# Queries and keys turned by the DMA engines' transpose instead of TensorE's, in a one-core transformer block

## The chip, the cores and the metric

The kernel runs on one core of a Trainium2 chip (trn2). The metric is the device time in microseconds of one execution. Before the change it was 766.03 us, the median of three runs (764.91 to 766.18). The core has five engines with instruction queues of their own: TensorE (PE, with its weight loads listed as PEld), VectorE (DVE), ScalarE (ACT), GpSimd (POOL) and SyncE (SP), which here only issues DMAs.

## The reference, cut to what matters

```python
x = x + 0.5 * ffn(layernorm(x))          # x: 8 x 512 x 128
x = x + attn(layernorm(x))
x = x + 0.5 * ffn(layernorm(x))
# attn: 16 heads of 64
q = rmsnorm(x @ Wq, q_rms_w);  k = rmsnorm(x @ Wk, k_rms_w);  v = x @ Wv
gate   = softplus(einsum('bthd,hd->bht', k, u / |u|) / sqrt(64))
bias   = -dist * softplus(omega) * slopes * gate         # causal
scores = q @ k.T / sqrt(64) + bias
y      = softmax(scores) @ v @ Wproj
```

`rmsnorm` divides each head's 64 numbers by their root mean square and multiplies them by a weight of 64 numbers.

## The kernel before, in words

The eight batches are worked off one after the other, each software-pipelined into the next. The order of the work on every engine is written out by hand in `ORDER` (line 27): one list per engine for the lead-in, the first batch, the six middle batches ("body", b = 1 to 6), and the last one. Each entry is a stage with its numbers and THIS, NEXT or LAST for the batch that it belongs to, so one body period works on three batches. An engine takes its own list strictly in order, and a wait at its head holds up all behind it. The stages of attention are grouped in four quarters (`qd`, four heads each) and four token blocks (`t`, 128 tokens).

To keep nearly full precision with 16-bit products, an operand is split into an upper part (rounded to 16 bits) and a lower part (what is left). `product` (lines 1087 to 1089) makes three matmuls of such pairs. PE's results of most stages go through a ring of four PSUM banks (`RING`); `taken_by` gives a bank back.

The way of queries and keys before:

- `qk`: PE projects one token block of a quarter, 512 columns. ACT squares it (L975) and copies it in 32 bits to `qkn` (L976), which gives the bank back; DVE sums the squares per head (L1551). `qkn` holds two quarters, eight blocks.
- `qkn`: ACT takes logarithm and exponential to get one over the root (L984, L987); POOL multiplies (L869).
- `t`: PE transposes with the 32-bit identity (`turn_heads`, L1200), 16 transposes of 128x128 for two banks of queries and two of keys per quarter. ACT writes the upper parts times the RMS weights into `qk2` (`hi_parts`, L1023), DVE subtracts for the lower parts (`lo_parts`, L1576), both reading PSUM. There are eight `t` stages per batch, eight transposes each.
- SP then copies by DMA: `rows` puts the upper parts into `qk1` (`place_upper`, L652, two of 256 KB a quarter), `swap` and `back` (L750, L751, L755, L756, four of 128 KB a quarter) arrange both halves of `qk2`.
- `gr`/`gd`/`nm` bring the gate rows and the negated row maxima into `qk1`. `a` (L1218, DVE L1586) finds row maxima, `s` (L1244 to L1246, ACT L1048) makes scores and exponentials.
- `pl`: POOL makes the lower part of the exponentials (L843); in the last batch DVE makes one of three (L1500). `pv` is the product with the values, DVE divides by the sums (L1601), ACT and POOL split it (`yt`, L1063, L847), and SP turns it by a DMA transpose (L766, 256 KB each, one per pair of heads).

Elsewhere DVE subtracts with both inputs in SBUF at a few places: L1434 (32 rows of the normed input), L1490 (hidden layer in the first and last feed-forward) and L1500. Its other large operations, L1576 and L1608 among them, read one input from PSUM. In the lead-in POOL makes the bias rows (`b2`, L892 to L897) and the diagonal of `u` (`ud`, L830).

```python
def place_upper(eng, qd, n):
    eng.dma_start(qk1[0:D, qd, n, :, :, :], qk2[n * D:(n + 1) * D, qd, K1:Q0 + 1, :, :])
# lo_parts, DVE, for each of queries and keys, 128 x 512, bank in PSUM
scalar_tensor_tensor(qk2[..LOWER..], bank, w, qk2[..UPPER..], ALU.mult, ALU.subtract)
# exponentials_lo, for comparison: both inputs in SBUF
tensor_tensor(pt_l[..], pt[..], pt_h[..], ALU.subtract)
```

Of the kernel before, what the change touches and what calls it, by code (L numbers as in the profile page):

```python
# [6 lines left out]
ALU = mybir.AluOpType  # L7
# [27 lines left out]
            ("t", 3, NEXT), ("qk", 2, 1, NEXT), ("qk", 2, 2, NEXT), ("a", 0, NEXT), ("qk", 2, 3, NEXT),
            ("a", 1, NEXT), ("qk", 3, 0, NEXT), ("a", 2, NEXT), ("a", 3, NEXT), ("v", 0, 2, NEXT), ("qk", 3, 1, NEXT),
            ("nm", 0, NEXT), ("qk", 3, 2, NEXT), ("a", 4, NEXT), ("v", 0, 3, NEXT), ("qk", 3, 3, NEXT),
            ("a", 5, NEXT), ("s", 0, NEXT), ("a", 6, NEXT), ("s", 1, NEXT), ("gl", 1, NEXT), ("a", 7, NEXT),
            ("t", 4, NEXT), ("v", 1, 0, NEXT), ("nm", 1, NEXT), ("pv", 0, NEXT), ("t", 5, NEXT), ("t", 6, NEXT),
        ],  # L40
        "first": [
            ("s", 2, THIS), ("t", 7, THIS), ("gr", 1, THIS), ("pv", 1, THIS), ("v", 1, 1, THIS), ("s", 3, THIS),
            ("pv", 2, THIS), ("a", 8, THIS), ("s", 4, THIS), ("a", 9, THIS), ("pv", 3, THIS), ("zt", "a", NEXT),
            ("s", 5, THIS), ("m", "a", NEXT), ("pv", 4, THIS), ("a", 10, THIS), ("s", 6, THIS), ("a", 11, THIS),
            ("h", "a", NEXT), ("nm", 2, THIS), ("wp", 0, THIS), ("pv", 5, THIS), ("out", "a", NEXT),
            ("v", 1, 2, THIS), ("s", 7, THIS), ("v", 1, 3, THIS), ("s", 8, THIS), ("a", 12, THIS),
            ("zt", "att", NEXT), ("pv", 6, THIS), ("a", 13, THIS), ("qk", 0, 0, NEXT), ("qk", 0, 1, NEXT),
            ("qk", 0, 2, NEXT), ("qk", 0, 3, NEXT), ("pv", 7, THIS), ("s", 9, THIS), ("a", 14, THIS),
            ("qk", 1, 0, NEXT), ("pv", 8, THIS), ("a", 15, THIS), ("qk", 1, 1, NEXT), ("v", 0, 0, NEXT),
            ("v", 0, 1, NEXT), ("qk", 1, 2, NEXT), ("qk", 1, 3, NEXT), ("pv", 9, THIS), ("gl", 0, NEXT),  # L50
            ("nm", 3, THIS), ("v", 0, 2, NEXT), ("wp", 1, THIS), ("t", 0, NEXT), ("t", 1, NEXT), ("s", 10, THIS),
            ("v", 0, 3, NEXT), ("gr", 0, NEXT), ("s", 11, THIS), ("t", 2, NEXT), ("t", 3, NEXT), ("s", 12, THIS),
            ("pv", 10, THIS), ("a", 0, NEXT), ("qk", 2, 0, NEXT), ("pv", 11, THIS), ("a", 1, NEXT), ("s", 13, THIS),
            ("a", 2, NEXT), ("qk", 2, 1, NEXT), ("qk", 2, 2, NEXT), ("pv", 12, THIS), ("a", 3, NEXT),
            ("qk", 2, 3, NEXT), ("qk", 3, 0, NEXT), ("s", 14, THIS), ("a", 4, NEXT), ("qk", 3, 1, NEXT),
            ("pv", 13, THIS), ("nm", 0, NEXT), ("qk", 3, 2, NEXT), ("a", 5, NEXT), ("s", 15, THIS),
            ("qk", 3, 3, NEXT), ("wp", 2, THIS), ("a", 6, NEXT), ("gl", 1, NEXT), ("pv", 14, THIS), ("a", 7, NEXT),
            ("t", 4, NEXT), ("nm", 1, NEXT), ("t", 5, NEXT), ("t", 6, NEXT),
        ],
        "body": [  # L60
            ("pv", 15, LAST), ("t", 7, THIS), ("s", 0, THIS), ("v", 1, 0, THIS), ("v", 1, 1, THIS), ("gr", 1, THIS),
            ("s", 1, THIS), ("v", 1, 2, THIS), ("s", 2, THIS), ("pv", 0, THIS), ("wp", 3, LAST), ("zt", "a", NEXT),
            ("pv", 1, THIS), ("s", 3, THIS), ("m", "a", NEXT), ("pv", 2, THIS), ("a", 8, THIS), ("s", 4, THIS),
            ("pv", 3, THIS), ("v", 1, 3, THIS), ("s", 5, THIS), ("a", 9, THIS), ("h", "a", NEXT), ("s", 6, THIS),
            ("a", 10, THIS), ("wp", 0, THIS), ("pv", 4, THIS), ("a", 11, THIS), ("out", "a", NEXT), ("nm", 2, THIS),
            ("zt", "c", LAST), ("pv", 5, THIS), ("s", 7, THIS), ("a", 12, THIS), ("pv", 6, THIS), ("s", 8, THIS),
            ("zt", "att", NEXT), ("pv", 7, THIS), ("a", 13, THIS), ("qk", 0, 0, NEXT), ("s", 9, THIS),
# [230 lines left out]
def macaron(nc: bass.Bass, x, Wq, Wk, Wv, Wproj, q_rms_w, k_rms_w, omega, u, W1, b1, W2, b2, scale, out):  # L298
# [23 lines left out]
    with ExitStack() as ctx:  # L322
# [147 lines left out]
        def q2(h):  # L470
            return qk2[:, h // QH, Q2[h % 2], h % QH // 2, :]
# [1172 lines left out]
```

## Time and profile before

| | |
|---|---|
| three runs | 764.91, 766.03, 766.18 us |
| the profiled execution | 766.36 us, of which the span from first to last instruction is 764.6 us |
| granted TensorE clock over the span | 0.991 of full |
| body | six periods of about 88.9 us |
| before the body | 75 us lead-in, then the first batch |

The profile gives for each engine the time in which an instruction of it ran (busy), for groups of equal instructions their number, mean duration and the idle time ahead of them, and for stretches of the span the same sums. Engines pipeline: an instruction's duration can overlap the next one's, so start-to-start distances in the timeline are what an instruction costs its engine when it is followed at once.

### The profile page before, as it was taken

The page shows a single profiled execution, that of the slowest core. Times are in us where ns is not written, and L with a number is a line of the kernel's source. Part 1 is how long each engine was busy: PE and PEld are TensorE (multiplying, and loading weights), DVE is VectorE, ACT ScalarE, POOL GpSimd, SP SyncE. Part 2 cuts the span into 40 slices and gives each one's busy share as a digit, 9 for nine tenths or more (in the row PEclk, how much of TensorE's full clock was granted, in tenths as well). Part 3 has the DMA queues.
Part 4 walks back from the last instruction along what each step waited for, and adds up shares of the span by engine and source line. Part 5 has one row for each costly group of instructions (what it writes and reads, how often), then busy time and mean ns, then how long its engine had stood idle before and what let it go on. Part 6 is the DMA issues. An engine that isn't in the chain of part 4 may idle for free.

```text
span 764.6 us, 25092 instructions
## 1 busy us (share of the span) xinstructions
PE 734.0 (96%) x9298; PEld 528.4 (69%) x9298; DVE 660.0 (86%) x2105; ACT 640.4 (84%) x1420; POOL 645.3 (84%) x753
## 2 busy tenths in 40 slices
PE   4889999999999999999999999999999999999987
PEld 2455777677667777587667776577776876777765
DVE  8799878987989788887989879898898879899976
ACT  5687889888998889987998889988898889986673
POOL 6356879989998989989999899989899899997791
PEclk9799999999999999999999999999999999999999
DMA  7022513343243423454053432535134440534431
GB/s 200 13 67 48 126 31 87 84 86 86 44 112 72 85 60 71 91 108 100 3 126 72 86 86 44 113 72 107 38 76 95 99 99 16 113 72 101 98 44 30
DMA packets 99618, 60.33 MB, mean 79 GB/s; under 512 B 74622, under 2 KB 86400, under 8 KB 99496
## 3 DMA queue, kind: packets, MB, share of 16 engines
q1 hardware_dynamic: 99336, 58.19, 35.8%
q8 instruction: 75, 1.23, 0.7%
q10 hardware_dynamic: 160, 0.52, 0.2%
q14 instruction: 47, 0.39, 0.2%
HBM read 4.74 MB, written 2.10 MB: 9 GB/s over the span
## 4 chain that ended last, share of the span: by engine, by line
PE 73%; ACT 11%; DVE 9%; issue 3%; POOL 2%; DMA 1%; SPq 0%; DVEq 0%; ACTq 0%; POOLq 0%
PE ps L1087 13%; PE ps L1088 13%; PE ps L1089 13%; PE ps L1218 8%; PE ps L1244 7%; PE ps L1245 7%; PE ps L1200 5%; ACT qk L1023 3%; PE ps L1246 3%; ACT pt L1048 2%; DVE masked L1586 2%; PE ps L1104 1%; ACT hid L965 1%; POOL pt_l L843 1%; PE ps L1114 1%
## 5 line engine op out<-in xcount | busy, mean ns | idle before, releaser
L843 POOL TENSOR_TENSOR pt_l<-pt 128x512 f16<-128x512 f32 x366 | 321.5, 907 | 35.1 <-ACT pt L1048 33.4
L1586 DVE CUSTOM_DVE_ANT_0 masked<-ps,causal_row 128x512 f16<-128x512 f32 x448 | 192.1, 486 | 26.2 <-PE ps L1218 25.3
L1048 ACT ACTIVATE pt<-ps 128x512 f32<-128x512 f32 (+1 forms) x384 | 174.7, 535 | 17.5 <-PE ps L1246 14.5
L869 POOL TENSOR_TENSOR qkn<-qkn,rs 128x512 f32<-128x512 f32 x128 | 129.9, 1043 | 29.3 <-ACT rs L987 28.6
L1244 PE MATMUL ps<-qk 128*128 128x512 f16 (+3 forms) x512 | 146.7, 300 | 0.0
L1245 PE MATMUL ps<-qk 128*128 128x512 f16 (+3 forms) x512 | 146.6, 299 | 0.0
L1087 PE MATMUL ps<-v_buf,pt 128*128 128x65 f16 x1280 | 129.8, 194 | 2.6 <-POOL pt_l L843 1.2
L1088 PE MATMUL ps<-v_buf,pt 128*128 128x65 f16 x1280 | 129.8, 194 | 0.0
L1089 PE MATMUL ps<-v_buf,pt_l 128*128 128x65 f16 x1280 | 129.6, 194 | 0.0
L1087 PEld LDWEIGHTS ps<-v_buf,pt 128*128 128x128 bf16 x1280 | 118.0, 98 | 8.4 <-issue 4.9
L1088 PEld LDWEIGHTS ps<-v_buf,pt 128*128 128x128 bf16 x1280 | 117.5, 98 | 1.8
L1089 PEld LDWEIGHTS ps<-v_buf,pt_l 128*128 128x128 f16 x1280 | 117.5, 97 | 0.0
L1246 PE MATMUL ps<-causal_t,ident 128*128 128x128 f16 x512 | 105.7, 219 | 0.0
L1218 PE MATMUL ps<-qk 96*128 96x512 f16 (+3 forms) x512 | 97.0, 300 | 1.8 <-ACT qkn L976 0.5
L847 POOL TENSOR_TENSOR ytt<-ytok,ytt 128x512 f16<-128x512 f32 x63 | 74.1, 1177 | 19.9 <-ACT ytt L1063 18.4
L975 ACT ACTIVATE sq<-ps 128x512 f32<-128x512 f32 x128 | 77.6, 606 | 13.7 <-PE ps L1089 13.1
L1551 DVE TENSOR_REDUCE ss<-sq 128x8 f32<-128x512 f32 x128 | 82.8, 679 | 5.4 <-ACT sq L975 5.2
L976 ACT ACTIVATE qkn<-ps 128x512 f32<-128x512 f32 x128 | 78.2, 611 | 0.0
L1087 PE MATMUL ps<-wqkv_h,zt_h_att 128*128 128x512 f16 x192 | 74.1, 386 | 4.0 <-DVE qk L1576 1.9
L1088 PE MATMUL ps<-wqkv_l,zt_h_att 128*128 128x512 f16 x192 | 73.8, 384 | 0.0
L1089 PE MATMUL ps<-wqkv_h,zt_l_att 128*128 128x512 f16 x192 | 73.6, 384 | 0.0
L1218 PEld LDWEIGHTS ps<-qk 96*128 96x128 f16 x512 | 44.1, 97 | 40.0 <-issue 4.4
(212 smaller groups left out, 1968.8 us busy)
## 6 DMA issues: line engine op xcount, KB each, us to landing
qk<-qk SPq DMA_DIRECT2D x128, 128.0 KB, 2.4
qk<-qk SPq DMA_DIRECT2D x62, 256.0 KB, 3.7
x_in<-in_L_attn_x SPq DMA_DIRECT2D x8, 256.0 KB, 3.0
out<-x_out SPq DMA_DIRECT2D x7, 256.0 KB, 2.4
qk<-qk SPq DMA_DIRECT2D x1, 1024.0 KB, 8.1
qk<-gtt SPq DMA_DIRECT2D x64, 8.0 KB
qk<-nmt SPq DMA_DIRECT2D x64, 2.0 KB
y_hl<-ytt SPq DMA_TRANSPOSE x62, 3.2
```

The lines of the kernel that those rows point to most:

```text
L843: g.tensor_tensor(pt_l[:, h % 2, c], pt[:, h % 2, c], pt_h[:, h % 2, c], ALU.subtract).then_inc(s_pt_l, 1)
L869: g.tensor_tensor(qk, qk, r.unsqueeze(4).broadcast_to([P, 2, 2, 2, D]), ALU.mult).then_inc(s_qkn, 1)
L1048: a.activation(pt[:, h % 2, c], ps[:, j, 0:width], ACT.Exp).then_inc(s_exp, 1)
L1087: pe.matmul(dst, ah, bh, start=first, stop=False)
L1088: pe.matmul(dst, ah, bl, start=False, stop=False)
L1089: return pe.matmul(dst, al, bh, start=False, stop=last)
L1218: mm = pe.matmul(dst, q1(h)[0:MROW, ib * P:keys], k1(h)[0:MROW, 0:keys], start=True, stop=by_dve)
L1244: pe.matmul(dst, k1(h)[:, keys], q1(h)[:, kb * P:T], start=True, stop=False)
L1245: pe.matmul(dst, k2(h)[:, keys], q2(h)[:, kb * P:T], start=False, stop=False)
L1246: mm = pe.matmul(dst[:, 0:P], ident16[:, :], causal_t16[:, :], start=False, stop=True)
L1551: d.tensor_reduce(ss[:, :, qd % 2, t, :], sq[:, blk % 4, :].rearrange("p (j m d) -> p j m d", j=2, d=D), AX.X, ALU.add).then_inc(s_sqsum, 1)
L1586: ins = d.tensor_tensor_reduce(masked[:, part.unit(s, i)[0], col:col + (ib + 1) * P], part.bank(s, i)[:, col:col + (ib + 1) * P], causal_r ...
```

## The change

Queries and keys are split while they still lie by token, and DMA transposes bring them into the layout by head.

- ACT still squares the whole bank; it then copies the queries' half only (256 columns, scaled by 1/16). DVE multiplies the keys' half by the product of both RMS weights (they only meet in the dot product) into the same tile and gives the bank back.
- `qkn` holds 5 token blocks instead of 8; ACT's copy waits for the lower part of the block five before.
- POOL multiplies as before. ACT then copies `qkn` to 16 bits (upper), DVE subtracts from `qkn` for the lower part: four of each per quarter, as before, now with all inputs in SBUF. They go to `qk_hl`, 128 x 1024 per block in the order lower query, upper query, upper key, lower key.
- SP turns each block with one DMA transpose of 256 KB into `qk2`, which thereby has both arrangements; `swap` and `back` are gone. `rows` is four DMAs of 128 KB a quarter.
- PE's `t` stages (512 transposes) are gone, with their 128 uses of ring banks.
- All five orders are new. In the lead-in the 512-column matmuls that only keep PE busy are 10, 3 and 6 instead of 8 and 10 (6 more stay), POOL makes `b2` ahead of `m`, and `ud` waits for DVE's L1490.

The diff, cut to its core:

```diff
@@ vector order, body, second half @@
-            ("v", 0, 1, NEXT), ("gl", 0, NEXT), ("v", 0, 2, NEXT), ("pv", 9, THIS), ("t", 0, NEXT), ("t", 1, NEXT),
-            ("pv", 10, THIS), ("wp", 1, THIS), ("t", 2, NEXT), ("gr", 0, NEXT), ("v", 0, 3, NEXT), ("pv", 11, THIS),
+            ("qk", 0, 2, NEXT), ("qk", 0, 3, NEXT), ("pv", 8, THIS), ("a", 15, THIS), ("t", 0, NEXT),
+            ("qk", 1, 0, NEXT), ("qk", 1, 1, NEXT), ("m", "c", LAST), ("t", 1, NEXT), ("qk", 1, 2, NEXT),
...
@@ gpsimd order, lead @@
-            ("ul", NEXT), ("clear", NEXT), ("m", "a", NEXT), ("b2", NEXT), ("ud", NEXT), ("wvl", NEXT), ("wol", NEXT),
+            ("ul", NEXT), ("b2", NEXT), ("m", "a", NEXT), ("clear", NEXT), ("ud", NEXT), ("wvl", NEXT),
...
@@ sync order, body @@
+            ("ln1", "a", NEXT), ("gd", 2, THIS), ("rows", 2, THIS), ("yt", 7, LAST), ("tq", 6, THIS), ("tq", 7, THIS),
+            ("gd", 3, THIS), ("yt", 0, THIS), ("yt", 1, THIS), ("rows", 3, THIS), ("nm", 2, THIS), ("yt", 2, THIS),
+            ("yt", 3, THIS), ("nm", 3, THIS), ("tq", 0, NEXT), ("tq", 1, NEXT), ("rows", 0, NEXT), ("gd", 0, NEXT),
+            ("tq", 2, NEXT), ("tq", 3, NEXT), ("gd", 1, NEXT), ("yt", 4, THIS), ("rows", 1, NEXT), ("yt", 5, THIS),
+            ("tq", 4, NEXT), ("add", "c", LAST), ("nm", 0, NEXT), ("tq", 5, NEXT), ("yt", 6, THIS), ("nm", 1, NEXT),
...
-        qkn = sb("qkn", [P, 2, 4, 2, T // 2])
+        TOKENS = 5
+        qkn = sb("qkn", [P, TOKENS, 512])
+        qk_hl = sb("qk_hl", [P, TB, 2 * 512], F16)
...
-        def place_upper(eng, qd, n):
-            eng.dma_start(qk1[0:D, qd, n, :, :, :], qk2[n * D:(n + 1) * D, qd, K1:Q0 + 1, :, :]).then_inc(s_upper[qd % 2], 16)
+        def place_upper(eng, b, qd, j):
+            for t in range(TB):
+                eng.wait_ge(s_qk_turned[t], (b * 4 + qd + 1) * 16)
+            side, rows = ((HI_LO, slice(0, D)), (LO_HI, slice(D, P)))[j]
+            for n in range(2):
+                eng.dma_start(qk1[0:D, qd, n, j, :, :], qk2[rows, qd, n::2, side, :]).then_inc(s_upper[qd % 2], 16)
...
+            def turn_qk(part, s, b, p):
...
+                if b > 0:
+                    sp.wait_ge(s_s_ps, ((b - 1) * H + (qd + 1) * QH) * 3)
+                for t in (2 * th, 2 * th + 1):
+                    sp.wait_ge(s_lo, block_of(b, qd, t) + 1)
+                    sp.dma_start_transpose(qk2[:, qd, :, :, t * P:(t + 1) * P].rearrange("p m j c -> p (m j) c"),
+                                           qk_hl[:, t, :]).then_inc(s_qk_turned[t], 16)
...
             def diagonal_u(part, s, b):
                 pool.wait_ge(s_u_unit, 1)
+                pool.wait_ge(s_hid_l_dve, FB)
...
             def take_qk(part, s, b, qd, t):
...
-                part.taken_by(a.activation(tokens(qd, t), part.bank(s).rearrange("p (j i n) -> p j i n", j=2, i=2), ACT.Copy), s)
+                if blk >= TOKENS:
+                    act.wait_ge(s_lo, blk - TOKENS + 1)
+                a.activation(of_q_and_k(tokens(blk), 0), part.bank(s)[:, 0:256].rearrange("p (m d) -> p m d", d=D),
+                             ACT.Copy, scale=1.0 / QKV_UP).then_inc(s_q_out, 1)
...
             def hi_parts(part, s, b, p):
...
+                    a.activation(upper(t), tokens(blk).rearrange("p (m f) -> p m f", m=QH), ACT.Copy).then_inc(s_hi, 1)
...
             def square_sums(part, s, b, qd, t):
...
+                dve.wait_ge(s_q_out, blk + 1)
+                part.taken_by(d.tensor_tensor(of_q_and_k(tokens(blk), 1), part.bank(s)[:, 256:512].rearrange("p (m d) -> p m d", d=D),
+                                              kw[:, :].unsqueeze(1).broadcast_to([P, QH, D]), ALU.mult), s)
...
             def lo_parts(part, s, b, p):
...
+                    dve.wait_ge(s_hi, blk + 1)
+                    d.tensor_tensor(lower(t), tokens(blk).rearrange("p (m j d) -> p m j d", m=QH, j=2),
+                                    upper(t).rearrange("p m (j d) -> p m j d", j=2), ALU.subtract).then_inc(s_lo, 1)
```

## Rows read from the trace of the kernel before

**Rows 1.** The page's busy shares of the whole span.

```profile
PE 734.0 (96%) x9298; PEld 528.4 (69%) x9298; DVE 660.0 (86%) x2105; ACT 640.4 (84%) x1420; POOL 645.3 (84%) x753
```

**Rows 2.** Busy time by stretch, five body periods; then the sum over them.

```profile
core 0: us, PE busy (x) PEld busy (x) DVE busy (x) ACT busy (x) POOL busy (x), PEclk, DMA share, GB/s
254.75:344.07 89.32, 88.42 (x1154) 64.05 (x1151) 77.15 (x261) 79.22 (x180) 81.13 (x93) 1.00 0.41 79
...
sum 444.29, PE 441.94 PEld 320.26 DVE 385.88 ACT 395.94 POOL 404.74; mean PE 88.39 PEld 64.05 DVE 77.18 ACT 79.19 POOL 80.95
```

**Rows 3.** Who waited for whom in those five periods: PE, DVE and POOL.

```profile
PE ps L1087 <- DMA y_hl<-ytt: 0.6, 1, 0.6
...
DVE masked L1586 <- PE ps L1218: 21.0, 35, 1.6
...
POOL pt_l L843 <- ACT pt L1048: 17.8, 25, 1.3
```

**Rows 4.** Busy time of line L1200 alone (PE's transposes) in the same five periods.

```profile
166.06:610.35 444.29, 41.66 (x320) 34.31 (x320) 1.00 0.38 80
```

**Rows 5.** Groups of ACT instructions by line: busy, mean ns.

```profile
L976 ACT ACTIVATE qkn<-ps 128x512 f32<-128x512 f32 x128 | 78.2, 611 | 0.0
...
L1063 ACT ACTIVATE ytt<-ytok 128x512 f16<-128x512 f32 x63 | 39.7, 631 | 3.8 <-DVE ytok L1601 3.3
...
L1023 ACT ACTIVATE qk<-ps,qws 128x512 f16<-128x512 f32 x64 | 45.0, 704 | 6.0 <-PE ps L1200 5.6
...
L952 ACT ACTIVATE zt_h_att<-ps 128x256 f16<-128x256 f32 x16 | 5.2, 376 | 0.0
```

**Rows 6.** DVE's timeline: start us, us; the distances of starts are what counts.

```profile
421.24 0.42 DVE L1601 TENSOR_TENSOR ytok<-ps,rden 128x256 f32<-128x256 f32 x1
421.58 0.74 DVE L1576 SCALAR_TENSOR_TENSOR qk<-ps,qws,qk 128x512 f16<-128x512 f32 x1
422.24 0.74 DVE L1576 SCALAR_TENSOR_TENSOR qk<-ps,kws,qk 128x512 f16<-128x512 f32 x1
```

**Rows 7.** DVE subtractions by line: ns min/median/max; L1500 and L1434 read SBUF twice.

```profile
L1500 DVE TENSOR_TENSOR pt_l<-pt x18: 681/967/1523, 690.3 to 740.5; 128x512 f16<-128x512 f32 x17, 128x256 f16<-128x256 f32 x1
...
L1434 DVE TENSOR_TENSOR z_hl<-z_a,z_hl x16: 281/282/697, 8.1 to 752.3; 32x128 f16<-32x128 f32 x16
...
L1608 DVE TENSOR_TENSOR v_buf<-ps,v_buf x64: 656/684/695, 42.1 to 710.3; 128x512 f16<-128x512 f32 x64
```

**Rows 8.** Timeline of POOL, then DVE, in the last batch: an overlap, and one without.

```profile
730.53 2.06 POOL L843 TENSOR_TENSOR pt_l<-pt 128x512 f16<-128x512 f32 x2 [0.39 <-ACT pt L1048]
...
702.72 1.61 POOL L843 TENSOR_TENSOR pt_l<-pt 128x512 f16<-128x512 f32 x2 [0.69 <-ACT pt L1048]
...
731.02 1.10 DVE L1500 TENSOR_TENSOR pt_l<-pt 128x512 f16<-128x512 f32 x1 [0.27 <-ACT pt L1048]
...
738.18 3.13 DVE L1500 TENSOR_TENSOR pt_l<-pt 128x512 f16<-128x512 f32 x3
```

**Rows 9.** Busy time by stretch, the part of the last batch with L1500.

```profile
690.00:742.00 52.00, 50.07 (x802) 38.54 (x800) 47.83 (x143) 35.65 (x77) 41.65 (x40) 1.00 0.41 82
```

**Rows 10.** The group of L1500 over the span: busy, mean ns.

```profile
L1500 DVE TENSOR_TENSOR pt_l<-pt 128x512 f16<-128x512 f32 (+1 forms) x18 | 16.9, 949 | 1.1 <-ACT pt L1048 1.1
```

**Rows 11.** SP's timeline: what issuing a transpose, and two copies, takes.

```profile
426.77 1.24 SPq L766 DMA_TRANSPOSE y_hl<-ytt  x1
428.06 1.23 SPq L652 DMA_DIRECT2D qk<-qk  x2
```

**Rows 12.** The page's DMA issues: count, KB each, median us from issue to landing.

```profile
qk<-qk SPq DMA_DIRECT2D x128, 128.0 KB, 2.4
qk<-qk SPq DMA_DIRECT2D x62, 256.0 KB, 3.7
...
y_hl<-ytt SPq DMA_TRANSPOSE x62, 3.2
```

**Rows 13.** DVE's and POOL's timeline in the lead-in.

```profile
17.34 5.12 DVE L1490 TENSOR_TENSOR hid_l<-hid 128x512 f16<-128x512 f32 x4 [1.16 <-ACT hid L965]
...
18.48 2.23 POOL L830 TENSOR_TENSOR pt<-usq,ident 16x1024 f32<-16x1024 f32 x1
```

More of the change, by code:

```diff
@@ L35 @@
[L35 to L39, printed above, removed]
+            ("out", "a", NEXT), ("warm", 1, 10, NEXT), ("zt", "att", NEXT), ("warm", 1, 3, NEXT), ("qk", 0, 0, NEXT),
@@ L783, in store @@
                         sp.dma_start(rows[:, TB // 2:TB, :], x_out[:, TB // 2:TB, :]).then_inc(s_out, 16)
[L785 removed]
+            run(ORDER["sync"], {"weights": load_weights, "clear": constant_rows, "ln1": load_x, "rows": place_operands, "gd": place_gates, "tq": turn_qk, "yt": turn_y, "nm": max_rows, "add": store})
             sp.wait_ge(s_out, 16 * (B + 1))
@@ L1016, in hi_parts, with place_queries @@
             def hi_parts(part, s, b, p):
-                if b == 0 and p == 0:
-                    act.wait_ge(s_prepared, 1)
-                    act.wait_ge(s_wv_lo, 1)
-                    act.wait_ge(s_wp_lo, 1)
-                for j, w in enumerate((qws, kws)):
-                    part.full(act, s, j)
-                    a.activation(qk2[:, p // 2, UPPER[j], p % 2, :], part.bank(s, j), ACT.Identity, scale=w[:, :]).then_inc(s_hi, 1)
-            def place_odd_heads(part, s, b, qd):
+                qd, th = p // 2, p % 2
+                for t in (2 * th, 2 * th + 1):
+                    blk = block_of(b, qd, t)
+                    act.wait_ge(s_qkn, blk + 1)
+                    if blk >= TB:
+                        act.wait_ge(s_qk_turned[t], (b * 4 + qd) * 16)
+                    a.activation(upper(t), tokens(blk).rearrange("p (m f) -> p m f", m=QH), ACT.Copy).then_inc(s_hi, 1)
+            def place_queries(part, s, b, qd):
                 if b == 0 and qd < 2:
@@ L1192, in gate_rows @@
                                             gt[:, :, :, :, :].rearrange("p s r i t -> p (s r i t)"), ident16[:, :]), s)
-            def turn_heads(part, s, b, p):
-                pe.wait_ge(s_qkn, (b * 4 + p // 2 + 1) * TB)
-                for j in range(2):
-                    part.room(pe, s, j)
-                    for t in range(TB):
-                        mm = pe.transpose(part.bank(s, j)[:, t * P:(t + 1) * P],
-                                          tokens(p // 2, t)[:, j, p % 2, :], ident[:, :])
-                    part.filled_by(mm, s, j)
             def max_scores(part, s, b, h):
```

474 lines of the change are left out of this document (235 added, 239 removed).

## The prediction

> **What bounds the kernel now.** I read the busy shares first: PE works 96% of the span, the other three 84 to 86% [rows 1]. The share is a mean over stages, so I cut the body into its periods. One lasts 88.86 us (444.29 over five), and in it PE is busy 88.39 us, POOL 80.95, ACT 79.19, DVE 77.18 [rows 2]. PE idles half a microsecond per period. The waits agree: in five periods one wait of PE itself counts, 0.6 us, while DVE waits 21 us for PE's maxima and POOL 17.8 us for exponentials that in turn wait for PE [rows 3]. So PE sets the pace, and whatever leaves PE is worth its time until the next engine is full. The reader should see how near that is: POOL has 7.9 us of room in a period, DVE 11.7.
>
> **What leaves PE.** The transposes keep it busy 41.66 us in five periods, 8.33 each (64 of 0.13 us) [rows 4]. PE's load falls to 80.1 us. The ring of banks has 16 uses fewer per batch; the bank of a `qk` stage is held about as long as before (square, a shorter copy, then DVE's 0.34 us), so I cost the ring at nothing.
>
> **ACT.** Per block it loses a copy of 0.611 us and an upper part of 0.704 us from PSUM, and gets a copy of 256 columns, like the 0.376 us one, and a cast from SBUF, like the 0.631 us one [rows 5]. That is 0.31 us less for each of 16 blocks, 4.9 us; ACT falls to 74.3. It now also waits at a copy for the lower part of five blocks before, with exponentials queued behind it. DVE's lists put the lower parts within five blocks of their own, so I add nothing, and keep it for the upper end.
>
> **DVE.** By distances of starts, the old lower part costs 0.66 us and a product of 256 columns 0.34 us [rows 6]. Out go 16 x 0.66 = 10.6 us; in come 16 x 0.34 = 5.4 us for the keys and 16 x 0.60 = 9.6 us for the new lower part (0.68 us alone, less the same 0.08 us of overlap as in those rows). Undisturbed, DVE rises from 77.2 to 81.7 us. That would leave the change a large gain.
>
> **The term that decides.** The new lower part reads SBUF twice, the old one read PSUM once. Compare DVE's subtractions of equal size: with one input in PSUM (L1608) 64 of them lie between 0.656 and 0.695 us, with POOL busy all the while. With both in SBUF (L1500) they lie between 0.681 and 1.523, median 0.967, and the small L1434 goes from 0.281 to 0.697 [rows 7]. The timeline shows against what: where POOL works, DVE's instruction takes 1.10 us, and POOL's pair of instructions, 1.61 us when undisturbed, takes 2.06; three such DVE instructions in a row take 3.13 us [rows 8]. So DVE waits until POOL's instruction is through, then POOL's next is held for 0.45 us; a second DVE instruction right behind finds POOL's next already in and waits again.
> The Trainium skill (SBUF — State Buffer, "Who interferes with whom") states this as a rule against this change: a DVE instruction with two SBUF inputs contends with a GpSimd one that reads SBUF, and the second to come is blocked until the first is finished. The rows agree on DVE's side; of the 0.68 us they show POOL losing 0.45. By the full 0.68 POOL would need 80.95 + 16 x 0.68 = 91.8 us.
>
> Price for DVE, per lower part: the low end is the mean of all 18, 0.949 - 0.681 = 0.27 us [rows 7, 10], measured where POOL was busy 80% (41.65 of 52.00) [rows 9] against 91% in the body. The high end is the longest, 1.523 - 0.681 = 0.84 us [rows 7]. The lower parts come in pairs, the second ready behind the first: I take 0.33 us for the first (0.27 scaled by POOL's higher share) and 0.67 for the second (near the high end, less where ACT has not yet made its upper part), mean 0.50. DVE: 81.7 + 16 x 0.50 = 89.7 us. POOL: 80.95 + 16 x 0.45 = 88.2 us. Both stand about where the period is today, 88.86 us, so PE's 8.3 us are bought with two engines that are full. The engine that bounds will not be without idle time: PE had 0.5 us, but its suppliers had 8 to 12 us of room. DVE's would have 1.5 (POOL), so I give it 1 us. Period 90.7 us, 1.8 more. Seven such periods (six of the body and the first batch, whose load is alike) make +13 us.
>
> **SP and the DMA queues.** Issuing a transpose takes 1.24 us, two copies 1.23 [rows 11]. A period has 16 transposes more (20 us), 8 copies more for `rows` (5) and 16 fewer of `swap` and `back` (10): SP issues some 15 us more, to about 50 of 88.9 us, by my count of its list. In the engines 16 transposes, 256 KB and 3.2 us each to landing, replace 16 copies of 128 KB at 2.4 us [rows 12]. Even if each kept all 16 engines for its whole landing time, 51 us of a period, with a DMA share of 0.38 to 0.41 now [rows 2], the sum would stay under full. On the path of a quarter stand 3.2 + 1.24 us of transposes and two more issues, some 5.7 us. PE's list has ten stages and more between the last projection of a quarter and its first maxima, and these cover it; the wait on the last batch's scores comes long after those. In a middle case this costs nothing; without cover it is 5.7 us a quarter.
>
> **Lead-in and end.** In the lead-in DVE's four hidden lower parts take 5.12 us while POOL makes the diagonal [rows 13]; undisturbed 4 x 0.60 + 0.08 = 2.5. The new wait puts that away, 2.6 us off a chain on which little else happens. Against it the first maxima wait for 4 to 6 us of transposes, in place of PE's transposes and, before the scores, of `swap` and `back`. I take -2.6, between -6 and +5. The end has none of the changed stages but `t` 7: nothing.
>
> **Sum.** 764.6 + 12.6 - 2.6 = 774.6 us of span. The profiled execution took 766.36 us, 1.8 around its span and 0.3 above the median of the runs. That makes 776.4, and against the median 776.
>
> **Rivals.** (1) *POOL's port has just room enough, and it is faster.* If lower parts mostly fall where POOL or DVE would have idled anyway, DVE is no bound and the floor is POOL's 88.2 us. It decides from 81.7 + 16w + 1 < 88.86, a mean wait w under 0.39 us, well inside my 0.27 to 0.84. Then -0.7 x 7 = -5, lead-in -3: 758, down to 755 with the lead-in at its best. For it: ACT and PE get room, so POOL's waits for exponentials shrink. Against it: POOL would have to be 99% busy, every period. Chance 0.27, 0.02 of it within 0.2% of today. (2) *The new instructions don't collide*, whatever L1500 did: DVE at 81.7 + 1 = 82.7 us, -6.2 x 7 - 3 = 720. Nothing in the rows speaks for it; 0.04. (3) *Each of a pair waits for a whole POOL instruction*: DVE 81.7 + 16 x 0.84 = 95.1 us at most; halfway from 90.7, a period of 92.8, +3.9 x 7 - 2.6 = 791. That is also about where the skill's full block of POOL, 91.8 and 1 idle, leads. Chance 0.12. (4) *Late quarters*: one of four uncovered in each period, 5.7 x 7 = +40, 804. SP takes its list in order, so a late lower part also holds y's transposes and the maxima behind it; 0.05. The forecast itself, 765 to 785, has 0.52, of which 0.05 within 0.2%.
>
> **The numbers.** A measurement of this kernel can tell 0.2%, 1.5 us, from no change. Faster: 0.25 + 0.04 = 0.29. The same: 0.07. Slower: 0.47 + 0.12 + 0.05 = 0.64. The range reaches from rival 1's low end to within rival 3: 753 to 796. It leaves out rivals 2 and 4, some of 3 and a little of 1, under 0.2 in all. Most of the slower cases alone lie between 768 and 794.
>
> **What would show each step.** PE busy near 80 us in a period, its idle time now several us, ended by DVE or POOL. The new lower part on DVE with a minimum of 0.68 and a mean near 1.18 us, the product of keys at 0.42 without spread. Some 16 POOL instructions a period 0.45 us longer than their like, as the pair of 2.06 against 1.61 us [rows 8]. DVE busy 98% of the body, POOL 96%. ACT near 74 us. L1490's four in 2.5 us. I am wrong if the lower parts stay at 0.68 us (rival 2), if DVE is under 95% busy while PE waits for a landing (rival 4), or if POOL's collisions are far fewer than 16 a period (rival 1).

## The result, and the profile after

The changed kernel takes 837.71 us (median of four runs, 835.62 to 841.32) against 765.47 for the kernel before in the same comparison: a ratio of 1.0948, 95% interval 1.0908 to 1.0988. It is 72 us slower, where 10 had been forecast and 796 was the upper end of the range. The profiled execution took 841.32 us with a span of 839.5 at a granted clock of 0.957 of the full 2.4 GHz.

The busy shares and the chain of waits, from the page of the changed kernel:

```profile
PE 720.5 (86%) x8787; PEld 486.9 (58%) x8787; DVE 749.3 (89%) x2232; ACT 621.3 (74%) x1421; POOL 692.5 (82%) x753
...
DVE 48%; PE 34%; issue 6%; ACT 4%; POOL 3%; DMA 3%; SPq 1%; DVEq 0%; ACTq 0%; POOLq 0%
```

Five body periods, each cut at the moment at which SP issues the load of the next input, from the busy time by stretch (PE, PEld, DVE, ACT, POOL, then granted clock, DMA share, GB/s):

```profile
269.72:366.03 96.31, 86.05 (x1086) 58.58 (x1084) 88.49 (x278) 76.78 (x178) 87.51 (x93) 0.98 0.50 95
...
464.07:562.40 98.33, 88.38 (x1086) 60.76 (x1084) 88.48 (x278) 76.96 (x179) 87.84 (x93) 0.95 0.53 94
...
sum 486.12, PE 432.70 PEld 295.02 DVE 442.05 ACT 384.77 POOL 437.39; mean PE 86.54 PEld 59.00 DVE 88.41 ACT 76.95 POOL 87.48
```

Cut in the same way, the kernel before has periods of 88.9 us, with PE 88.3, DVE 77.0, ACT 79.2 and POOL 81.1 (its [rows 2] were cut some 10 us later in the period and differ by 0.2 at most). In the changed kernel DVE is busy 88.4 us a period (forecast 89.7), POOL 87.5 (88.2), ACT 77.0 (74.3). Yet the period is 97.2 us (486.12 over five), not 90.7. No engine is full: DVE idles 8.8 us, POOL 9.7, PE 10.7. The reader should stop here: the two loads that were forecast came out within 1.3 us, and the period is 6.5 us longer than the sum made of them.

By line, DVE's new lower part, its product of the keys, and POOL's multiplication (ns, minimum, median and maximum); then a collision in the timeline (start us, us):

```profile
L1592 DVE TENSOR_TENSOR qk_hl<-qkn,qk_hl x128: 675/1098/1610, 37.7 to 763.3; 128x512 f16<-128x512 f32 x128
L1565 DVE TENSOR_TENSOR qkn<-ps,kw x128: 405/411/426, 29.3 to 748.3; 128x256 f32<-128x256 f32 x128
L889 POOL TENSOR_TENSOR qkn<-qkn,rs x128: 1047/1058/1522, 33.6 to 753.1; 128x512 f32<-128x512 f32 x128
```

```profile
314.69 3.00 DVE L1592 TENSOR_TENSOR qk_hl<-qkn,qk_hl 128x512 f16<-128x512 f32 x2
...
313.38 1.17 POOL L866 TENSOR_TENSOR ytt<-ytok,ytt 128x512 f16<-128x512 f32 x1
314.61 2.52 POOL L889 TENSOR_TENSOR qkn<-qkn,rs 128x512 f32<-128x512 f32 x2
```

The lower part has its minimum at 0.675 us and reaches 1.61; two of them take 3.00 us where POOL's pair takes 2.52 instead of the 2.08 that two lone multiplications take elsewhere. The product of the keys (L1565) has no spread at 0.41 us. The idle time, in the same five periods (us, times, longest):

```profile
ACT nmt L1078 <- PE ps L1238: 21.7, 10, 4.8
ACT qkn L998 <- DVE qk_hl L1592: 14.6, 20, 1.0
...
DVE rden L1613 <- PE ps L1111: 13.3, 10, 2.0
DVE x L1544 <- PE ps L1111: 9.5, 5, 1.9
...
PE ps L1136 <- DVE qkn L1565: 9.3, 5, 1.9
PE ps L1109 <- DVE qkn L1565: 8.0, 10, 1.4
PE ps L1230 <- DVE qkn L1565: 8.0, 15, 0.7
```

PE now waits 25.3 us for banks that DVE gives back after the keys' product (L1565), and ACT waits 14.6 us at the copy into the five-block buffer for a lower part. Before, PE's waits came to 0.6 us [rows 3]. DVE's waits for PE are no longer than they were: 22.8 us in the two groups shown and some 11 more in smaller ones, against 21.0 at the maxima [rows 3] and some 18 more in smaller groups before. What is new beside the banks is ACT's wait of 21.7 us for the turned row maxima (L1078), which was 2.2 us. It is still 16.6 us in a_free below, whose periods are as short as before, so by itself it need not lengthen a period.

Where the 74.9 us of span are, by the moment at which SP issues the load of each next input: lead-in 80.3 against 75.2 us (+5.1), the first batch 92.9 against 81.0 (+11.9), the five periods 486.1 against 444.6 (+41.6), everything after 180.2 against 163.8 (+16.4). The last figure holds the sixth body period too. If that one grew like the others, by 8 to 10 us, the last batch is left with 6 to 8; this split is an estimate from the other periods. So every stage with the changed work in it is longer, and the lead-in too, though its collision did go: L1490's four (now L1502) take 2.50 us for 5.12 [rows 13], and the first sums of squares start 2.8 us earlier (29.7 against 32.5), but the first exponentials 5.0 us later (72.2 against 67.2). Between these two points PE stands 4.7 us once at the first maxima for a copy of gate rows, and ACT 7.8 us for transposes that free `qk_hl`. One trace of each is not exact to the microsecond here: in kernels below whose lead-in is that of before, the first exponentials start between 64.7 (b_less_pool) and 67.3 us (b_half_v_turns).

### The profile page after: what moved, and what is told of

The parts are those of the page before. It is cut to its first block, busy times and chain, and to the rows that moved or that the text cites. A ratio compares the mean times of both kernels' runs of the same rounds, so it can differ in the third digit from the quotient of the medians.

```text
span 839.5 us, 24423 instructions
## 1 busy us (share of the span) xinstructions
PE 720.5 (86%) x8787; PEld 486.9 (58%) x8787; DVE 749.3 (89%) x2232; ACT 621.3 (74%) x1421; POOL 692.5 (82%) x753
## 3 DMA queue, kind: packets, MB, share of 16 engines
q8 instruction: 70, 1.15, 0.6%
## 4 chain that ended last, share of the span: by engine, by line
DVE 48%; PE 34%; issue 6%; ACT 4%; POOL 3%; DMA 3%; SPq 1%; DVEq 0%; ACTq 0%; POOLq 0%
DVE qk_hl L1592 12%; DVE masked L1602 10%; DVE ss L1568 8%; PE ps L1109 7%; PE ps L1111 6%; PE ps L1110 6%; DVE qkn L1565 4%; PE ps L1230 4%; PE ps L1255 3%; PE ps L1256 3%; DVE ytok L1617 3%; POOL pt_l L862 2%; DMA qk<-qk_hl 1%; PE ps L1126 1%; PE ps L1257 1%
## 5 line engine op out<-in xcount | busy, mean ns | idle before, releaser
L862 POOL TENSOR_TENSOR pt_l<-pt 128x512 f16<-128x512 f32 x366 | 344.0, 967 | 45.9 <-ACT pt L1070 45.7
L889 POOL TENSOR_TENSOR qkn<-qkn,rs 128x512 f32<-128x512 f32 x128 | 143.8, 1144 | 45.6 <-ACT rs L1010 44.6
L1109 PE MATMUL ps<-v_buf,pt 128*128 128x65 f16 x1280 | 135.0, 196 | 16.5 <-DVE ytok L1617 12.3
L1592 DVE TENSOR_TENSOR qk_hl<-qkn,qk_hl 128x512 f16<-128x512 f32 x128 | 142.1, 1148 | 2.7 <-ACT qk_hl L1046 2.6
L1109 PEld LDWEIGHTS ps<-v_buf,pt 128*128 128x128 bf16 x1280 | 121.0, 100 | 30.0 <-issue 20.2
L1110 PE MATMUL ps<-v_buf,pt 128*128 128x65 f16 x1280 | 135.0, 196 | 0.0
L1111 PE MATMUL ps<-v_buf,pt_l 128*128 128x65 f16 x1280 | 134.9, 196 | 0.0
L1230 PE MATMUL ps<-qk 96*128 96x512 f16 (+3 forms) x512 | 106.3, 318 | 24.7 <-DVE qkn L1565 12.7
L1110 PEld LDWEIGHTS ps<-v_buf,pt 128*128 128x128 bf16 x1280 | 120.6, 100 | 2.2
L1111 PEld LDWEIGHTS ps<-v_buf,pt_l 128*128 128x128 f16 x1280 | 120.5, 99 | 0.0
L1568 DVE TENSOR_REDUCE ss<-sq 128x8 f32<-128x512 f32 x128 | 86.0, 672 | 0.0
L1046 ACT ACTIVATE qk_hl<-qkn 128x512 f16<-128x512 f32 x128 | 75.6, 632 | 14.1 <-DMA qk<-qk_hl 7.8
L1230 PEld LDWEIGHTS ps<-qk 96*128 96x128 f16 x512 | 45.1, 101 | 67.3 <-issue 22.4
```

The source lines that it names most:

```text
L862: g.tensor_tensor(pt_l[:, h % 2, c], pt[:, h % 2, c], pt_h[:, h % 2, c], ALU.subtract).then_inc(s_pt_l, 1)
L889: g.tensor_tensor(qk, qk, r.unsqueeze(3).broadcast_to([P, QH, 2, D]), ALU.mult).then_inc(s_qkn, 1)
L1109: pe.matmul(dst, ah, bh, start=first, stop=False)
L1110: pe.matmul(dst, ah, bl, start=False, stop=False)
L1111: return pe.matmul(dst, al, bh, start=False, stop=last)
L1230: mm = pe.matmul(dst, q1(h)[0:MROW, ib * P:keys], k1(h)[0:MROW, 0:keys], start=True, stop=by_dve)
```

## The experiments

Theory A is the prediction's: DVE and POOL are full through collisions, and the period follows the fullest. Rivals: the bank that DVE gives back late; the DMA transposes' latency; the new orders; and later, that a period is no engine's load. Times are medians; each ratio is against the kernel before run beside it. The medians of that kernel lie between 763.5 and 765.7 us from one comparison to the next, so a difference of 2 us between two variants from different comparisons says nothing. Kernels made from the one before begin with b, from the changed one with a.

### Undoing parts of the change

```diff
# a_reduce_lo: DVE's lower part becomes a reduction of one input, no collision
-  d.tensor_tensor(lower(t), tokens(blk)..., upper(t)..., ALU.subtract)
+  d.tensor_reduce(<unused>, tokens(blk)..., AX.X, ALU.add)
# a_act_bank: ACT copies queries and keys and gives the bank back; DVE's product
# becomes a reduction of equal size that only POOL waits for
-  a.activation(of_q_and_k(tokens(blk), 0), part.bank(s)[:, 0:256]...)
+  part.taken_by(a.activation(tokens(blk)..., part.bank(s)...), s)
# a_both: both edits
# a_no_turn: no DMA transpose from the second batch on
+  if b == 0:
       sp.dma_start_transpose(qk2[...], qk_hl[:, t, :])
```

> The changed kernel with DVE's lower part (two inputs in SBUF) replaced by a sum over the same 512 numbers of the token block alone: one input in SBUF, 0.67 us like the other sums, same place, same waits. It leaves out the lower parts of queries and keys. If the collisions with POOL are the cause: DVE's load per body period falls from 88.4 to about 81.5 us, POOL's from 87.5 to 81, the period from 97.2 to 89 to 90, the time from 838 to 775 to 785. If the banks given back by DVE are: DVE and PE still wait for each other, the period stays above 93, the time at 810 to 825. If the DMA transposes come late: above 825.

> The changed kernel, but ACT copies all 512 columns of a qk bank and gives it back; DVE's instruction on 256 columns stays as a load of about the same length, but reads the keys' half of the token block in SBUF (a sum, one input), and POOL waits for it as before. It leaves out the RMS weights of the keys. The lower part still collides. If the collisions are the cause, the time stays within 825 to 840, since both engines keep their loads. If the banks given back by DVE are, PE's waits for that product (some 5 us a period) go and the time falls to 790 to 810.

> Both edits together (no lower parts, no weights of the keys). If the two causes explain the loss: DVE near 81.5 us per period, ACT near 79, and a period of 84 to 87, time 735 to 760. If the time stays above 800, the cause is neither: the transposes' path, the ring of five token blocks, or the orders themselves.

> The changed kernel without its DMA transposes from batch 1 on: SP waits as before for each lower part and for the scores, issues nothing, and what waited for a landing waits for the lower part instead. It leaves out the turning of queries and keys in batches 1 to 7, which then use those of batch 0. If the transposes' latency, their share of the DMA engines or SP's time are the cause, the time falls below 800. If the collisions or the banks are, it stays within 825 to 840.

What waited for a transpose that a_no_turn leaves out waits for the lower part instead. a_reduce_lo and a_both fill `qk_hl` with zeros once, on DVE in the lead-in.

Measured: a_reduce_lo 789.77 us, ratio 1.0314 (1.0264 to 1.0364); a_act_bank 845.74, 1.1068 (1.1034 to 1.1103); a_both 790.5, 1.0338 (1.0308 to 1.0367); a_no_turn 837.17, 1.0958 (1.0925 to 1.0991).

Taking the collisions away wins 48 us of the 72, though the 790 lies between what the two theories gave (775 to 785, and 810 to 825), and a_both, forecast at 735 to 760 or above 800, lies in neither. That DVE hands the bank back is not the main cause: with ACT doing it, PE's waits for L1565 are gone, but it now waits for other banks that come back late from DVE (14.0 us for L1623, 11.4 for the maxima L1601, in five periods), and the time is 8 us longer. The edit also puts 2.6 us a period more on ACT (79.6 for 77.0), so it does not show that the hand-back costs nothing. Transposes, with their issues on SP and their share of the queues, are worth nothing while the collisions are there. Without collisions, in a_reduce_lo:

```profile
sum 457.00, PE 420.15 PEld 287.69 DVE 403.01 ACT 380.27 POOL 407.42; mean PE 84.03 PEld 57.54 DVE 80.60 ACT 76.05 POOL 81.48
...
PE ps L1230 <- DMA qk<-qk: 10.4, 6, 2.9
```

Every engine is under 85 us and the period 91.4, still 2.5 longer than before. PE's maxima now wait for the copies of the upper parts, which come behind the transposes.

### Adding the suspected loads to the kernel before

```diff
# b_collide: the lower part reads its first input from SBUF (other values)
-  scalar_tensor_tensor(qk2[..LOWER..], part.bank(s, j), w[:, :], ...)
+  scalar_tensor_tensor(qk2[..LOWER..], w1s[:, :], w[:, :], ...)
# b_keys_op: 0.34 us of DVE work more per block, one input, its result unused
   dve.wait_ge(s_sq, blk + 1)
+  d.tensor_reduce(<unused>, w1s[:, 0:256]..., AX.X, ALU.add)
# b_loads: both
```

> The kernel before with only its lower part of queries and keys (L1576) reading a constant in SBUF instead of the PSUM bank, so both inputs in SBUF, same size, place and waits. It leaves out the true lower parts. PE keeps its transposes, and the order is that of before. If collisions cost DVE some 0.4 to 0.5 us and POOL 0.45 us each: DVE from 77.0 to about 83, POOL from 81.1 to about 88 us per period, the two still at or below the period of 88.9, and the coupled waits make it longer: 785 to 810. If collisions only hurt where the order has no room, this one has 8 to 12 us of it, and the time stays under 775.

> The kernel before with one more DVE instruction per token block of queries and keys, a sum of 256 numbers of a constant in SBUF, 0.34 us of DVE each, 5.4 us a period, one input, no collision, nobody waits for it. The output is whole. If DVE's load alone is the cause, the time rises by 15 us or more; if it is hidden in DVE's 11.9 us of idle time, by under 8 us.

> Both edits in the kernel before (it leaves out the true lower parts): DVE near 88 and POOL near 88 us per period, as in the changed kernel, but with PE's transposes, the old ring and the old order. If the loads and collisions make the changed kernel slow, this one is as slow or slower, 830 or more, for PE has 8 us more to do. If the new orders are at fault, it stays under 815.

Measured: b_collide 796.18, 1.0388 (1.0356 to 1.042); b_keys_op 796.72, 1.0408 (1.0379 to 1.0438); b_loads 823.15, 1.0746 (1.0718 to 1.0774). The sums of the five periods of b_collide and of b_keys_op:

```profile
sum 464.71, PE 450.28 PEld 320.04 DVE 407.60 ACT 401.73 POOL 436.51; mean PE 90.06 PEld 64.01 DVE 81.52 ACT 80.34 POOL 87.30
```

```profile
sum 464.05, PE 448.66 PEld 321.19 DVE 409.29 ACT 397.96 POOL 406.45; mean PE 89.73 PEld 64.24 DVE 81.86 ACT 79.59 POOL 81.29
```

The collisions alone cost the old order 31 us. b_keys_op is the sharper case: DVE idled 11.9 us a period, gets 4.8 us more, and is left with 11; the period grows by 3.9 us. Nobody waits for the result of the added instruction, but it stands in DVE's list right ahead of the sum of squares, and ACT waits for that sum:

```profile
ACT ssl L984 <- DVE ss L1552: 24.5, 20, 2.8
```

In the kernel before this wait was 5.8 us (5 times, L1551). The 18.7 us more in five periods are 3.7 a period, as much as the period grew. So DVE's idle time was not room at this place. That the wait is the whole cause is not shown: no run put the same work behind the sum. In b_collide that wait stays at 5.8 us, and PE waits instead, 11.2 us in five periods, for banks that L1576 gives back. And b_loads carries nearly the changed kernel's DVE and POOL loads (85.8 and 86.7 us a period) with none of its orders, transposes or buffers, and has 58 us of the 72. Its 823 lies between the two forecasts (830 or more for the loads, under 815 for the orders).

### The keys' product, with and without collisions

```diff
# a_no_keys: ACT copies the whole bank and gives it back, DVE's product is gone
-  part.taken_by(d.tensor_tensor(of_q_and_k(tokens(blk), 1), ..., kw..., ALU.mult), s)
# a_light: a_no_keys and a_reduce_lo together
```

> The changed kernel without DVE's product for the keys: ACT copies all 512 columns and gives the bank back; the lower part still collides. It leaves out the RMS weights of the keys. In the kernel before an added DVE load of 5.4 us a period cost 31 us. If a DVE microsecond costs the same here, the time falls by 20 to 31 us, to 807 to 818. If the order, not the load, makes the loss, by under 10 us.

> As a_no_keys, and the lower part is the sum with one input in SBUF: no collisions, no product. DVE near 75.5 us per period, PE near 81, ACT 79, POOL 81, all at or under the kernel before. It leaves out the lower parts and the keys' weights. If DVE's load and the collisions are the whole loss, what PE lost must now show: 735 to 755. If the new orders or the longer path of a quarter cost as well, the time stays at 760 or above.

Measured: a_no_keys 818.63, 1.0694 (1.0661 to 1.0728); a_light 787.18, 1.0284 (1.0246 to 1.0322). The product costs 19 us beside collisions (838 to 819) and 3, hardly more than the spread between comparisons, without them (790 to 787). The collisions alone cost 31 us (819 to 787), as in the old order, and 48 beside the product. In a_light no engine carries over 0.5 us more than before (PE 83.3, DVE 76.3, ACT 79.0, POOL 81.6) and it still takes 22 us more.

### Is PE the bound?

```diff
# b_fewer_turns: one transpose of four
-  for t in range(TB):
+  for t in range(1):
       mm = pe.transpose(part.bank(s, j)[:, t * P:(t + 1) * P], ...)
# a_pe_fill: one matmul per head done twice
   for kb in blocks:
+      if kb == 0: pe.matmul(dst, k1(h)[:, keys], q1(h)[:, kb * P:T], start=True, stop=True)
       pe.matmul(dst, k1(h)[:, keys], q1(h)[:, kb * P:T], start=True, stop=False)
```

> The kernel before with one of each four transposes of PE's t stages, 16 a period instead of 64: PE's load falls by some 6.2 us a period, all else alike. It leaves out three quarters of the turned queries and keys. If PE alone bounds the kernel before, as the prediction had it, the period falls by 6, the time by 40 to 45 us, to 720 to 726. If DVE, ACT and POOL are as tight in the static order, by less than half of that.

> The changed kernel with the first matmul of each head's scores issued twice (512 columns, 16 a period, some 3.4 us of PE); the output is whole. The granted clock averages 0.97 in the body now and was 1.00. If PE's idle time and its lower clock drive the loss, more work for PE changes nothing or helps: 825 to 840. If PE is in the loop with DVE all the same, each microsecond costs: 845 to 860.

Measured: b_fewer_turns 765.26 us, 1.0003 (0.9984 to 1.0021), ten runs; a_pe_fill 846.13, 1.1062 (1.103 to 1.1095). The sum over b_fewer_turns' periods, then its transposes alone:

```profile
sum 444.80, PE 428.76 PEld 296.48 DVE 386.29 ACT 395.72 POOL 405.63; mean PE 85.75 PEld 59.30 DVE 77.26 ACT 79.14 POOL 81.13
```

```profile
155.64:600.44 444.80, 20.69 (x80) 10.36 (x80) 1.00 0.36 80
```

Two things are to be seen. A quarter of the transposes still holds half of their busy time, 20.69 of 41.66 us [rows 4]: the records of matmuls in a row overlap, so a lone one adds 0.26 us where four in a row add 0.13 each (one record has 0.28 us in the mean). And the 2.6 us a period that PE did lose turn into idle time; the period stays at 88.96. PE was 99% busy and was not what held the period. In the changed kernel, where PE idles 10.7 us a period, 3.8 us more of PE work a period cost 1.8, and 8.4 us of the time: idle time is not room there either, where the work stands right ahead of the exponentials.

The lower clock, 0.957 for 0.991 of 2.4 GHz, goes with PE's idle time: in the periods it is 1.00 in a_free and b_loads, where PE idles 5.3 and 5.6 us, and 0.95 to 0.98 in a_no_keys and the changed kernel, where it idles 9.2 and 10.7. It could stretch PE's 86.5 us by 3 a period at most. b_loads costs 58 us at 0.990, so the clock isn't the main cost; how much it adds in the changed kernel was not tried.

### What is left without collisions: the transposes, or the orders

```diff
# a_free: a_reduce_lo and a_no_turn;  a_light_free: a_light and a_no_turn
```

> Changed kernel without collisions (lower part a reduction of one input) and without the DMA transposes from the second batch on (what they would bring keeps the first batch's values). Against 790 with the transposes: theory A (the way of a quarter through the transposes, hidden behind the collisions until now, is on the path once these are gone: PE waited 10.4 us in five periods for the upper parts' DMAs): 775 to 783. Theory B (the new orders and not the transposes cost the rest): 787 to 791.

> Changed kernel without collisions, without the keys' product and without the DMA transposes from the second batch on: no new load on any engine, PE 5 us a period lighter than before. Theory A (the transposes' way costs the remaining 22 us): 765 to 772, of it 5 us in the lead-in. Theory B (the orders do): 783 to 788.

Measured: a_free 775.1, 1.0139 (1.0103 to 1.0175); a_light_free 777.33, 1.0156 (1.0139 to 1.0173). a_free's periods:

```profile
sum 443.65, PE 416.89 PEld 286.48 DVE 402.89 ACT 379.55 POOL 407.39; mean PE 83.38 PEld 57.30 DVE 80.58 ACT 75.91 POOL 81.48
```

With the collisions gone, the transposes are worth 15 us (790 to 775), 2.7 a period (91.4 to 88.7); while the collisions were there, nothing. Their latency, their issues on SP and their share of the DMA engines went together, so which of these it is stays open. The body of a_free has the period of before, 88.7 us, with PE 4.9 us lighter, ACT 3.3 lighter and DVE 3.6 heavier. Its span is 8.0 us over the one before: 5.5 in the lead-in, 1.8 in the first batch, 1.6 after the periods, 0.9 less within them. Theory A's 775 to 783 held. For a_light_free it gave 765 to 772, and that missed, as did theory B's 783 to 788: without the keys' product nothing more is won.

### Less work in the kernel before

```diff
# b_half_lo, b_half_v_turns, b_less_pool, b_less_all: from the second batch on,
# 256 of 512 columns for
#   b_half_lo       DVE's lower part of queries and keys
#   b_half_v_turns  DVE's lower part of the values; and b_fewer_turns' edit
#   b_less_pool     POOL's lower parts of y and of the hidden layer
#   b_less_all      b_half_v_turns, b_less_pool, and ACT's square
-  part.bank(s, j)            # b_half_lo, the others alike
+  part.bank(s, j)[:, 0:n]    # n = T if b == 0 else T // 2
```

> Kernel before; from the second batch on DVE makes the lower part of queries and keys on 256 of 512 columns only (the other half keeps the values of the first batch). PE, ACT and POOL do what they did; DVE loses 16 x about 0.33 = 5.3 us a period, the mirror of the added keys operation, which cost 31 us. Theory A (PE sets the pace and its 0.5 us of idle time is all there is): at most 3 us faster, 762 to 766. Theory B (the static orders tie PE and DVE in one loop, so DVE's work is paid for at some 0.7 us of period per us): about 5.3 x 0.7 x 6 = 22 us faster, 743; PE's load of 88.4 us a period would forbid this unless PE's busy time shrinks too, which the records of PE would show. Between them: B only upwards, 765.

> Kernel before with PE making one of four transposes of queries and keys (as in the earlier run, which took the same time as before) and, from the second batch on, DVE making the values' lower part on 256 of 512 columns (8 x 0.33 = 2.6 us a period less). Theory A (PE was the bound, and the earlier run only moved the bound to DVE's and ACT's waits): with both lighter the time falls, to 745 to 755. Theory B (neither load is what sets the period; the latency of the chain between engines is): within 3 us of before, 762 to 768.

> Kernel before; from the second batch on POOL makes the lower parts of y and of the hidden layer on 256 of 512 columns (the rest keeps older values): 8 x about 0.5 and 4 to 8 x about 0.5, some 6 us a period less of its 81. Theory A (POOL is the hidden bound): 725 to 750. Theory B (no single load sets the period): 762 to 767.

> Kernel before with less on all four engines from the second batch on: POOL as in b_less_pool (about 6 us a period), ACT squares 256 of 512 columns (16 x about 0.23 = 3.7 us), DVE's lower part of the values on 256 columns (8 x 0.33 = 2.6 us), PE one transpose of four (6 us). Theory A (the period is the load of whichever engine is fullest, PE's busy time being partly waits): all loads fall by 3 to 7%, and the time with them, to 720 to 745. Theory B (each engine's list waits on the others' results one by one, and the sum of these latencies, not a load, is the period): only the shortened steps on that way count, a few us: 755 to 765.

Measured: b_half_lo 765.06, 0.9996 (0.9982 to 1.001); b_half_v_turns 764.73, 0.9995 (0.9981 to 1.0009); b_less_pool 763.22, 0.9986 (0.9974 to 0.9999); b_less_all 760.11, 0.995 (0.9933 to 0.9967). The periods of b_half_lo and of b_less_all:

```profile
sum 444.22, PE 440.95 PEld 320.07 DVE 368.97 ACT 395.21 POOL 405.68; mean PE 88.19 PEld 64.01 DVE 73.79 ACT 79.04 POOL 81.14
```

```profile
sum 440.75, PE 427.44 PEld 296.20 DVE 374.82 ACT 381.21 POOL 372.19; mean PE 85.49 PEld 59.24 DVE 74.96 ACT 76.24 POOL 74.44
```

The theory that DVE's work is paid for in both directions, 743 us for b_half_lo, is wrong: 5 us more cost 31, 3 us less bring nothing. With 2.8 us less on PE, 2.1 on DVE, 2.9 on ACT and 6.7 on POOL the period falls by 0.8 us, from 88.9 to 88.15. So no load of one engine is the period. What fits all runs is that the lists, each taken strictly in order, form several rounds of waits from engine to engine that are about equally long: a delay on any of them lengthens the period, a gain on some leaves the others. That is inferred from these runs. Where added delay surfaces is on record (ACT's wait for the sum of squares in b_keys_op, PE's for banks in b_collide); which rounds hold the 88.9 us was not found. None of these runs shortened SP's list or a DMA's latency, so a round through them is a rival that stands untested.

### The part worth keeping

```diff
# b_lead: the lead-in's POOL order and the wait of ud, taken over alone
-  ("ul", NEXT), ("clear", NEXT), ("m", "a", NEXT), ("b2", NEXT), ("ud", NEXT),
+  ("ul", NEXT), ("b2", NEXT), ("m", "a", NEXT), ("clear", NEXT), ("ud", NEXT),
   pool.wait_ge(s_u_unit, 1)
+  pool.wait_ge(s_hid_l_dve, FB)          # in diagonal_u
-  pool.wait_ge(s_w_l["a"], 1)            # in bias_rows
+  pool.wait_ge(s_unorm, 1)
```

> The kernel before with two details of the change's lead-in only: POOL makes the diagonal of u after DVE's hidden lower parts, and the bias rows before m. The output is whole. DVE's four hidden lower parts fall from 5.12 to about 2.5 us, the whole by 1 to 3 us, to about 0.997 of before. If that stretch is not on the chain that counts, no difference.

Measured: 763.24 us (12 runs), 0.9965 (0.995 to 0.9979). DVE's four lower parts and POOL's diagonal no longer overlap:

```profile
17.65 2.50 DVE L1491 TENSOR_TENSOR hid_l<-hid 128x512 f16<-128x512 f32 x4 [1.29 <-ACT hid L966]
...
20.28 2.75 POOL L831 TENSOR_TENSOR pt<-usq,ident 16x1024 f32<-16x1024 f32 x1 [2.14 <-issue]
```

DVE's 2.6 us are won at this place, and the periods are as before (444.4 us for five). The first exponentials start at 64.2 instead of 67.2 us, but with an untouched lead-in they started at 64.7 in b_less_pool, so that the gain is real rests on the times: 0.35%, with an interval of 0.2 to 0.5%. It is small, but this version is faster than both kernels.

## Why the prediction was wrong, step by step

- **"So PE sets the pace, and whatever leaves PE is worth its time until the next engine is full": this step failed.** PE was busy 88.39 of 88.86 us, but taking 2.6 us from it changes nothing (b_fewer_turns). It was read from a busy share, in which a lone transpose counts for twice what it takes in a row (0.26 for 0.13 us), and from PE's few waits.
- **"What leaves PE", 8.33 us, to 80.1.** PE is at 86.5 in the changed kernel. Part can be the clock (0.95 to 0.98 by period), and part the records: with both collisions and transposes gone, at a clock of 1.00, it is 83.4. Only 4.9 us left PE; the term was too large by 3 us.
- **"I give it 1 us. Period 90.7 us": this step failed, and it is the largest part of the error.** The loads under it were right: DVE 88.4 for 89.7, POOL 87.5 for 88.2. The idle time of the fullest engine is 8.8 us, not 1, and the period 97.2. Over six periods that is 39 of the 65 us by which the span was missed; the first batch has 10, the lead-in 8, and the last batch some 6 to 8. "DVE 11.7 us of room" was the same mistake: b_keys_op fills 4.8 us of it and pays 3.9 a period.
- **"The term that decides."** The mechanism was right. The lower part takes 1.148 us in the mean (142.1 us over 128), 0.47 above its minimum, for 0.50 forecast. POOL rises by 6.5 us a period, 0.41 per lower part, for 0.45. It decides, too: 48 us of the 72 go with it. The Trainium skill (SBUF — State Buffer, "Who interferes with whom") calls the pair of ports that VectorE and GpSimd share an exclusive lock. The runs agree on DVE's side (up to 0.94 us longer, beside POOL instructions of 1.05), and for POOL they show 0.41 in the mean and 0.48 at most (L889, 1.522 for 1.047) of the 0.68 us.
- **ACT**: 77.0 for 74.3. The durations were right (0.632 for 0.631, 0.386 for 0.376), but the old ones overlapped: the copies and upper parts fall from 168.3 to 125.0 us when their groups are added up, 43 us, while ACT's busy time falls by 19 (640.4 [rows 1] to 621.3). DVE's part of the sum was made from distances of starts, ACT's was not. The wait for the lower part of five blocks before was "nothing" and is 14.6 us in five periods; what that wait alone costs was not tried.
- **"I cost the ring at nothing."** PE waits 25.3 us in five periods for banks given back at L1565. But a_act_bank, which takes that away and puts 2.6 us a period on ACT, is no faster. The wait is mainly where the delay surfaces, not its cause; whether the hand-back costs a few microseconds is not shown.
- **SP and the transposes, "in a middle case this costs nothing"**: true in the changed kernel (a_no_turn, 837), and only because the collisions cover it. Without them it is 15 us, 2.7 a period; the prediction's 5.7 a quarter "without cover" did not come.
- **Lead-in.** The -2.6 us are there (29.7 for 32.5 at the first sums of squares), and b_lead shows them as 2.4 us of whole time. But the way from there to the first exponentials is 7.8 us longer, so the lead-in gives +5.1, the upper end. Which of the transposes, the new orders or fewer matmuls that keep PE busy (the clock of the lead-in is 0.87 for 0.91) does it was not tried. **"The end ... nothing"** is some 6 to 8 us; of all that follows the five periods, 16.4 us, a_free keeps 1.6.
- **The rivals.** None was it. Rival 4 (804) came nearest, and it alone took the time from a wait and not from a load; its wait, for the transposes, is ruled out by a_no_turn. Rivals 1 to 3 took the period from one engine's load, and that is why the range, whose upper end lies within rival 3, missed.
- **The signs.** "DVE busy 98% of the body, POOL 96%" came out as 91 and 90%. DVE under 95% was to mean rival 4, but PE's waits were for banks and not for a landing: the signs had no place for a period without a full engine.

The 72 us by the runs: collisions 48 (838 to 790), the transposes once these are gone 15 (790 to 775), and 10 to the kernel before, which in the trace lie outside the five periods. The shares depend on the order of removal; transposes first would have 0.

## What to carry to other kernels

In a kernel whose engines take hand-fitted lists in order, a share of 96 to 99% doesn't prove a bound and idle time doesn't prove room: before moving work, take a little from the supposed bound and add a little to the supposed spare engine, at the places in the lists where the change will, and price the change by those two slopes (here 0 us for 2.6 us less on PE, and 3.9 us a period for 4.8 more on DVE). That such slopes would have priced this change was not tried. An instruction whose result nobody needs still delays whatever stands behind it, so look who waits for that. Splitting an operand where both inputs lie in SBUF made each DVE instruction wait 0.47 us and POOL 0.41 here; keep such a subtraction on a PSUM source while POOL is loaded. A new cost that seems free may be covered by a larger one: take that away first, then ask again.

## What the runs showed of the hardware

- A DVE subtraction with both inputs in SBUF beside a POOL busy 90% took 0.675 to 1.61 us for 128x512 (128 of them, mean 1.15), and each cost POOL about 0.4 us; b_collide gives the same with a different instruction (mean 1.02 for 0.74 us, POOL +0.39). With one input in SBUF (a_reduce_lo, b_keys_op) POOL stays at 81.3 to 81.5 us a period.
- PE's busy time does not fall in step with the instructions taken out: 48 of 64 transposes a period removed, 2.6 us less busy of the 6.2 that their share of [rows 4] would give.
- ACT's instructions overlap in the same way: two groups of them fell by 43 us when their means are added up, ACT's busy time by 19 (640.4 to 621.3); before, two upper parts of 0.69 us started 0.59 us apart.
- A DMA transpose of 256 KB within SBUF took 3.3 us in the median from issue to landing in the changed kernel (128 of them).
